# A decoder with two mixture layers on one core: indirect transfers broken up by sums, first fetches from another queue, the ready table built earlier

## The reference, cut to what matters

```python
# layer 0: 16 experts, 4 groups; a token takes 4 experts out of its 2 best groups
scores = softmax(xt @ Wg.T)
weights = take_along_axis(scores, topi)
h = silu(xt @ W1[e].T) * (xt @ W3[e].T)          # inner width 176
y = sum over the 4 chosen e of weights[e] * (h @ W2[e].T)
z = (silu(xt @ Ws1.T) * (xt @ Ws3.T)) @ Ws2.T    # two shared experts, width 352
x = layernorm(x + y + z)
# layer 1: 8 experts, a token takes 2
probs = softmax(gelu(x @ rw1) @ rw2)
Ye = gelu(x @ w1[e] + b1[e]) @ w2[e] + b2[e]     # inner width 1024
Ce = gelu(b1[e]) @ w2[e] + b2[e]                 # where a token has not chosen e
x = layernorm(x + sum over k, e of probs_k * (Ye or Ce))
```

## Time and profile before

| | us |
|---|---|
| median of three runs | 1445.8 |
| profiled execution | 1446.67 |
| its span in the profile | 1444.8 |
| TensorE matmuls busy | 1157.7 (80%) |
| TensorE weight loads busy | 924.1 (64%) |
| ScalarE busy | 521.8 (36%) |
| VectorE busy | 489.7 (34%) |
| GpSimd busy | 419.5 (29%) |

### The profile page before, as it was taken

One profiled execution on the slowest core, in us unless ns is written; L12 is line 12 of the kernel. 1 busy time (PEld: TensorE's weight loads), 2 busy tenths in 40 slices (PEclk: granted clock), 3 DMA queues, 4 the chain that ended last, 5 costly groups with the idle time before them and its releaser, 6 DMA issues. The chain is left out here.

```text
span 1444.8 us, 29452 instructions
## 1 busy us (share of the span) xinstructions
PE 1157.7 (80%) x10340; PEld 924.1 (64%) x10341; DVE 489.7 (34%) x1215; ACT 521.8 (36%) x1308; POOL 419.5 (29%) x521
## 2 busy tenths in 40 slices
PE   4988889868695069899947888888763599999998
PEld 2666767756353047676736667676542598989997
DVE  1255543555641012222233444554327300000223
ACT  2324433334131023333315555665430243333342
POOL 2022121121237731477441444121105300020143
PEclk9888988967698579999979999999755899999999
DMA  4011059900433323454440000000017564555573
GB/s 137 16 45 30 16 197 352 341 2 1 177 109 109 113 63 115 120 149 141 131 148 1 17 17 16 2 2 1 1 42 306 184 215 151 180 178 176 165 242 117
DMA packets 106677, 163.44 MB, mean 113 GB/s; under 512 B 16816, under 2 KB 86048, under 8 KB 104864
## 3 DMA queue, kind: packets, MB, share of 16 engines
q1 hardware_dynamic: 83344, 124.41, 26.4%
q0 software_dynamic: 9696, 26.75, 5.8%
q10 hardware_dynamic: 13536, 10.83, 2.3%
HBM read 100.87 MB, written 61.08 MB: 112 GB/s over the span
## 5 line engine op out<-in xcount | busy, mean ns | idle before, releaser
L2220 PE MATMUL bank<-m_XGT,m_w 128*128 128x128 f32 x1248 | 153.6, 283 | 4.4 <-issue 2.2
L2220 PEld LDWEIGHTS bank<-m_XGT,m_w 128*128 128x128 f32 x1248 | 149.2, 199 | 6.1 <-issue 4.5
L2234 PE MATMUL bank<-m_w,m_HT 128*128 x624 | 141.2, 379 | 0.0
L2071 ACT ACTIVATE m_HT<-bank,m_b 128x128 f32<-128x128 f32 x312 | 89.0, 369 | 108.3 <-PE bank L2220 73.2
L2234 PEld LDWEIGHTS bank<-m_w,m_HT 128*128 128x128 f32 x624 | 115.9, 191 | 14.2
L1311 PE MATMUL bank<-m_W,m_XGT 128*128 x316 | 110.8, 474 | 3.7 <-issue 2.8
L1015 POOL DMA_INDIRECT GA<-ys,r_pos x64 | 62.2, 972 | 101.6 <-DVE m_Y L1253 76.3
L2031 POOL DMA_INDIRECT m_GA<-ys,r_pos x32 | 31.6, 989 | 177.2 <-SPq L1989 168.5
L1184 ACT ACTIVATE m_XGT<-bank 128x256 f32<-128x256 f32 x79 | 30.3, 383 | 120.1 <-DVE m_Y L1253 88.4
L1311 PEld LDWEIGHTS bank<-m_W,m_XGT 128*128 128x128 f32 x316 | 55.4, 195 | 23.0 <-issue 6.3
L1133 POOL DMA_INDIRECT xs<-X,r_pos x64 | 62.4, 975 | 25.6 <-issue 15.2
(11 more groups left out here) (345 smaller groups left out, 2398.9 us busy)
## 6 DMA issues: line engine op xcount, KB each, us to landing
m_w<-in_m_w SPq DMA_DIRECT2D x47, 1024.0 KB, 5.4
m_XG<-xs SPq DMA_DIRECT2D x118, 128.0 KB
xs<-zeros SPq DMA_DIRECT2D x1, 10112.0 KB, 33.6
ys<-zeros SPq DMA_DIRECT2D x1, 10112.0 KB, 49.8
ys<-m_Y ACTq DMA_DIRECT2D x79, 128.0 KB
m_W<-in_w SPq DMA_DIRECT2D x2, 2816.0 KB, 14.5
xs<-zeros SPq DMA_DIRECT2D x1, 4992.0 KB, 47.9
ys<-zeros SPq DMA_DIRECT2D x1, 4992.0 KB, 34.2
```

Source lines behind the costliest of these rows:

```text
L2071: last = nc.scalar.activation(HT[:, b % 2, at, :], BU[i][:, c * P:(c + 1) * P], ACT.Gelu, bias=b1[:, b % WB, at:at + 1])
L2220: last = nc.tensor.matmul(BU[i][:, c * P:(c + 1) * P], w1[:, b, m, lo:lo + P], XGT[:, b % 2, m * P:(m + 1) * P], start=m == 0, stop=m == K ...
L2234: last = nc.tensor.matmul(BY[b % 2][:, 0:DIM], HT[:, b % 2, c, :], w2[:, bass.ds(e, 1), c, :], start=c == 0, stop=c == CH - 1)
```

## The change

In the first mixture layer:

- The scatter is issued two transfers at a time. Behind each pair GpSimd adds half a `Z` tile (128 of 256 columns) of the token tile before; behind the first pair of a tile it first waits until the token tile before has landed. The eight whole additions behind the scatter go.
- The gather of tile t+1 is issued one fetch at a time, each ahead of one of the four weightings of tile t.
- ScalarE issues the fetches of slot tiles 0 to 6 (0 to 3 ahead of its first copy, 4 to 6 between its next steps). SyncE starts with number 7, looks at `in_place` for one slot tile in four up to number 39, and for all after that waits once for the whole scatter.
- The steps of the ready table lie between the last up products of the shared experts.

In the second: `LAG` is 1; ScalarE issues the weights of slot tiles 0 to 3 and the rows of 0 to 3; SyncE starts with rows 4 and 5 and looks at `in_place` only in the first 12 steps of its loop; TensorE waits for the weights of the down products (`ld_w2`) ahead of its loop.

The diff without its context (the hunk of `layer1`, in which only an argument of `fetch_rows` goes, is left out):

```diff
@@ -956 +956 @@
-    def ready_on_dve(self, nc, dve, ident, req_bank, ready_bank, ahead):
+    def ready_on_dve(self, nc, dve, ident, req_bank, ready_bank, ahead, fill=None, fills=((), ())):
@@ -968 +968 @@
         self.req_step = do.k
+        for i in fills[0]:
+            fill(i)
         dve.wait_ge(self.counted, 4)
...
         self.ready_step = do.k
+        for i in fills[1]:
+            fill(i)
         dve.wait_ge(self.counted, 5)
...
-    def ready_on_pe(self, nc, pe, ones, ident, req_bank, ready_bank):
+    def ready_on_pe(self, nc, pe, ones, ident, req_bank, ready_bank, between=None):
         pe.wait_ge(self.steps.sem, self.req_step)
         nc.tensor.transpose(req_bank[0:TILES, 0:P], self.req[:], ident[:]).then_inc(self.counted, 1)
+        if between:
+            between()
         pe.wait_ge(self.steps.sem, self.ready_step)
@@ -987 +993 @@
-def tile_pipeline(engine, step, n, visits=()):
-    done = 0
+def tile_pipeline(engine, step, n, visits=(), done=0):
     for at, visit in (*visits, (n - PEEL, None)):
@@ -1009 +1014 @@
-def fetch_rows(nc, pool, fx, t, done):
+def fetch_row(pool, fx, t, k, done):
+    pool.indirect_dma_start(
+        out=fx.GA[:, t % 2, k, :], out_offset=None, in_=fx.ys,
+        in_offset=bass.IndirectOffsetOnAxis(ap=fx.pos0[:, t, k:k + 1], axis=0)).then_inc(done, 16)
+def fetch_rows(pool, fx, t, done):
     for k in range(TOP0):
-        pool.indirect_dma_start(
-            out=fx.GA[:, t % 2, k, :], out_offset=None, in_=fx.ys,
-            in_offset=bass.IndirectOffsetOnAxis(ap=fx.pos0[:, t, k:k + 1], axis=0)).then_inc(done, 16)
-def add_rows(nc, pool, fx, t, own):
+        fetch_row(pool, fx, t, k, done)
+def add_rows(nc, pool, fx, t, own, fetch=None):
...
     for k in range(TOP0):
+        if fetch:
+            fetch(k)
         last = nc.gpsimd.tensor_scalar(rows[:, k], rows[:, k], fx.wt0[:, t, k:k + 1], 1.0, ALU.mult, ALU.mult)
@@ -1037 +1048 @@
     POOL_GATES = 2 * SC + 1
+    FIRST, CHECKED = 7, 32
     with ExitStack() as mem:
@@ -1087 +1099 @@
-                def slot(j):
-                    return sp.value_load(r.tslot[0:1, bass.ds(j, 1)], min_val=0, max_val=NT - 1)
-                def load(j, b):
-                    need, s = sp.value_load(r.tneed[0:1, bass.ds(j, 1)], min_val=1, max_val=TILES), slot(j)
+                def load(j, b, checked=None):
+                    if checked is not None:
+                        need = sp.value_load(r.tneed[0:1, bass.ds(checked, 1)], min_val=1, max_val=TILES)
+                    s = sp.value_load(r.tslot[0:1, bass.ds(j, 1)], min_val=0, max_val=NT - 1)
                     sp.wait_ge(t_full, j + 1)
-                    sp.wait_ge(in_place, need)
+                    if checked is not None:
+                        sp.wait_ge(in_place, need)
                     sp.dma_start(XG[:, b, :].unsqueeze(1), slots[:, bass.ds(s, 1), :]).then_inc(ld_x[b], 16)
-                for j in range(7):
+                load(FIRST, FIRST % 4, FIRST)
+                with sp.Fori(0, CHECKED // 4) as i:
+                    for b in range(4):
+                        load(i * 4 + (FIRST + 1 + b), b, i * 4 + (FIRST + 4) if b == 0 else None)
+                sp.wait_ge(in_place, TILES)
+                with sp.Fori(0, (NT - FIRST - 1 - CHECKED) // 4) as i:
+                    for b in range(4):
+                        load(i * 4 + (FIRST + 1 + CHECKED + b), b)
+                for j in range(NT - (NT - FIRST - 1) % 4, NT):
                     load(j, j % 4)
-                def step(j, b, ahead):
-                    if follows(ahead, 7):
-                        load(j + 7, (b + 3) % 4)
-                tile_pipeline(sp, step, NT)
                 for b in range(2):
@@ -1128 +1142 @@
+                def add_shared(t, half):
+                    part = fx.X[:, t, half * P:(half + 1) * P]
+                    pool.wait_ge(z_used, t // 2 + 1)
+                    nc.gpsimd.tensor_tensor(part, part, Z[:, t, half * P:(half + 1) * P], ALU.add).then_inc(z_added, 1)
                 for t in range(TILES):
...
                             in_=fx.X[:, t, :], in_offset=None).then_inc(sent[t % 2], 16)
-                    if t:
-                        landed(t - 1)
+                        if t and k == 1:
+                            landed(t - 1)
+                        if t and k % 2:
+                            add_shared(t - 1, k // 2)
                 landed(TILES - 1)
-                pool.wait_ge(z_used, PAIRS)
-                for p in range(PAIRS):
-                    nc.gpsimd.tensor_tensor(fx.X[:, pair_tiles(p), :], fx.X[:, pair_tiles(p), :], Z[:, pair_tiles(p), :],
-                                            ALU.add).then_inc(z_added, 1)
-                pool.wait_ge(z_added, PAIRS)
+                for half in range(2):
+                    add_shared(TILES - 1, half)
+                pool.wait_ge(z_added, 2 * TILES)
                 own = fx.pool_steps
-                def gather(t):
+                def may_fetch(t):
                     pool.wait_ge(y_used, pool.value_load(r.ready[0:1, t:t + 1], min_val=3, max_val=NT + 2))
                     pool.sem_inc(due, 1)
-                    fetch_rows(nc, pool, fx, t, gathered[t % 2])
+                def fetch(t, k):
+                    fetch_row(pool, fx, t, k, gathered[t % 2])
                 pool.wait_ge(r.placed, 3)
-                gather(0)
+                may_fetch(0)
+                for k in range(TOP0):
+                    fetch(0, k)
                 for t in range(EARLY):
                     if t + 1 < EARLY:
-                        gather(t + 1)
+                        may_fetch(t + 1)
                     pool.wait_ge(gathered[t % 2], 16 * TOP0 * (t // 2 + 1))
-                    add_rows(nc, pool, fx, t, own)
+                    add_rows(nc, pool, fx, t, own, (lambda k: fetch(t + 1, k)) if t + 1 < EARLY else None)
@@ -1206 +1229 @@
+                def load(j, b):
+                    need = act.value_load(r.tneed[0:1, j:j + 1], min_val=1, max_val=TILES)
+                    s = act.value_load(r.tslot[0:1, j:j + 1], min_val=0, max_val=NT - 1)
+                    act.wait_ge(t_full, j + 1)
+                    act.wait_ge(in_place, need)
+                    act.dma_start(XG[:, b, :].unsqueeze(1), slots[:, bass.ds(s, 1), :]).then_inc(ld_x[b], 16)
+                act.wait_ge(r.placed, 2)
+                for j in range(4):
+                    load(j, j)
                 rows(0, 0)
+                load(4, 0)
                 rows(1, 1)
+                load(5, 1)
                 silu(0, 0)
                 rows(2, 2)
+                load(6, 2)
                 silu(1, 1)
@@ -1235 +1271 @@
                                ((POOL_GATES, POOL_GATES + 1), (POOL_GATES + 2,)))
-                for n in range(POOL_GATES + 3, SC * GROUPS):
-                    gated(n)
-                r.ready_on_dve(nc, dve, fx.ident[:], BU[0], BU[1], 2)
+                r.ready_on_dve(nc, dve, fx.ident[:], BU[0], BU[1], 2, gated,
+                               ((POOL_GATES + 3,), (POOL_GATES + 4,)))
@@ -1289 +1323 @@
                 r.order_on_pe(nc, pe, fx.ones, BU[0], BU[1], lambda: shared_up(3, (0,)))
-                shared_up(3, (1, 2))
+                shared_up(3, (1,))
+                r.ready_on_pe(nc, pe, fx.ones, fx.ident, BU[0], BU[1], lambda: shared_up(3, (2,)))
                 shared_down(2)
                 shared_down(3)
-                r.ready_on_pe(nc, pe, fx.ones, fx.ident, BU[0], BU[1])
@@ -1903 +1937 @@
     E2 = 2 * E1
-    HC, WB = CH // 2, 4
-    AHEAD, LAG, POOL_WRITES = 2, 4, PAIRS - 2
+    HC, WB, CHECKED = CH // 2, 4, 12
+    AHEAD, LAG, POOL_WRITES = 2, 1, PAIRS - 2
     with ExitStack() as mem:
@@ -1960 +1994 @@
-                def load(j, b):
-                    need, s = sp.value_load(r.tneed[0:1, bass.ds(j, 1)], min_val=1, max_val=TILES), slot(j)
+                def load(j, b, checked):
+                    if checked:
+                        need = sp.value_load(r.tneed[0:1, bass.ds(j, 1)], min_val=1, max_val=TILES)
+                    s = slot(j)
                     sp.wait_ge(t_full, j + 1)
-                    sp.wait_ge(in_place, need)
+                    if checked:
+                        sp.wait_ge(in_place, need)
                     sp.dma_start(XG[:, b, :].unsqueeze(1), slots[:, bass.ds(s, 1), :]).then_inc(ld_x[b], 16)
-                def load_w1(j, b, freed=None):
+                def load_w1(j, b, freed):
                     e = sp.value_load(r.texp[0:1, bass.ds(j, 1)], min_val=0, max_val=E1 - 1)
-                    if freed is not None:
-                        sp.wait_ge(h_gelu, freed)
+                    sp.wait_ge(h_gelu, freed)
                     sp.dma_start(w1[:, b].unsqueeze(2), io["m1_w1"][:, :, bass.ds(e, 1), :]).then_inc(ld_w1[b], 16)
...
                 sp.wait_ge(r.placed, 2)
-                for j in range(WB):
-                    load_w1(j, j)
-                    for i in ((0, 1), (2, 3), (), (4, 5))[j]:
```

(36 more changed lines are left out.)

## The result

The changed kernel took 1382.09 us (median of 4 runs, 1380.47 to 1389.18) against 1445.15 (4 runs, 1440.53 to 1446.75): a ratio of 0.9587, 95% interval 0.955 to 0.9624. The forecast was 1380, range 1362 to 1424. The total was met; two terms of its sum were not, with opposite signs.

A forecast was written before the change was run, and what follows sets the result against it. The prediction took GpSimd's long unbroken runs of indirect transfers, which freeze the other engines, to bound the two mixture-layer dips. 1446.7 - 56 (first layer) - 10 (second layer) = 1380.7, so 1380 us, range 1362 to 1424.

The forecast's parts named there:

- The freeze is what ends last, and breaks lift it: Both layers' dips: GpSimd's long unbroken run of indirect transfers holds the other engines; breaking it frees them.
- TensorE without a hole between 450 and 517: First layer, beside the scatter: sign that would show the forecast true, TensorE working on without a gap.
- First Y at 471.8: First layer: the first Y comes at 471.8 us, 56 us earlier than before.
- A pair takes 3.1 us: First scatter: two transfers and half a sum take 3.1 us, 6.2 a token tile; the scatter ends near 525.5.
- Broken pairs cost 0.1 us a transfer, 4 us in all (0 to 21): First layer's loop beside the scatter: about 42 transfers slow the other engines by 0.1 us each.
- Alternating gathers give back 4 us: First layer's loop: the run of eight gathers goes, as fetches alternate with sums, 4 us less.
- Net 0 for the loop: First layer, first to last Y: 4 us lost beside the scatter and 4 us regained from the gathers cancel.
- rival of a slow ScalarE queue: First layer: ScalarE's four fetches take 45 us instead of 6.7, gain about 25, time 1418; chance 0.14.
- GpSimd has 12 us to spare: First layer: the fetch of tile 11 can start at 645.5, let go at 657.4, so GpSimd stays hidden.
- Second layer 10 us: Second layer's start: third up product at 1135.8 against 1146.05, 10 us earlier, bounds 0 and 18.
- The gathers of the second layer keep their 7.82 us: Second layer: its run of eight gathers is untouched, so its 7.82 us on the chain of waits stay.
- rival of another cause: Both dips: something other than GpSimd's run holds the engines, time stays near 1446; chance 0.04.

The follow-up runs named there:

- a1_scatter_run: Changed kernel with the first layer's 64 scatter transfers unbroken again and all half sums of Z behind them: 1415.19 us.
- c4_break_alone: Kernel before the change, only its first scatter broken: behind every two transfers half a sum of Z and a second sum of that size: 1390.10 us, ratio 0.961.
- the fours: Changed kernel with four transfers of the first scatter, then one whole sum of Z, instead of two and half a sum: 1400.32 us.
- a2_gather_run: Changed kernel with the four gathers of the next token tile in the first layer issued in one run ahead of the sums: 1409.74 us.
- c3_long_sync: The kernel with the long breaks, its first seven row fetches of the first layer on SyncE's queue, none on ScalarE's: 1368.69 us against 1367.46.
- the long breaks: Changed kernel with a second sum of the same size, into a spare tile, behind every half sum of Z in the first scatter: 1367.46 us.

## Why the prediction was right, step by step

- *The freeze is what ends last, and breaks lift it.* Right: shown by `a1_scatter_run` one way, `c4_break_alone` the other. At the change's own spacing they lift it only in part: the sign "TensorE without a hole between 450 and 517" failed, with 32.11 us busy of the 51 from 466 to 517.
- *First Y at 471.8.* It came at 466.3. Z was done at 448.85 (forecast 452.5), the fetches began at 450.40 (453.1) and took 5.87 us for four (6.7), and the first Y followed 10.05 us behind them (12).
- *A pair takes 3.1 us.* 2.90: the first transfer took 0.98 behind 0.17, the half sum 0.46. The scatter ended at 516.3, not 525.5. It made the spacing closer than forecast, which is the wrong side.
- *Broken pairs cost 0.1 us a transfer, 4 us in all (0 to 21).* This term failed. The price was 28.9 us in one profile and 34.7 in the other (nine steps of 5.66, six of 8.23, against 2.45). I took the row of eight transfers in a row as the nearest and then 0.1 without a row. That row was read too low as well: 2.8 + 2 us over eight are 0.6 each and not at most 0.5, and VectorE's Y beside those eight came some 8 us late in all. (By the 3.1 us a pair 54 us also hold 35 transfers, not 42.) What counts is the spacing over a long stretch, and a pair at 1.452 us a transfer is near the fours' 1.426, where a slot tile took 11.3 us. At 1.63 us the 0.1 would have been enough: 25 steps of 2.55 us lose 2.4 us.
- *Alternating gathers give back 4 us.* It was 17. Before, the loop took 208.9 us for 78 steps, 17.7 more than 2.45 each; `a2_gather_run` and `c4_break_alone` with runs of gathers lose 16.4 and 16.9 behind the scatter, the kernels without them 0.2 to 4.6. I had counted only the run of eight, and too low, and left out the runs of four, beside most of which a step took 1.3 to 1.5 us longer before.
- *Net 0 for the loop.* +11.4; with the first Y 5.5 earlier than forecast, the first layer gave 50 instead of 56.
- *ScalarE's queue.* The rival of a slow ScalarE queue didn't come: four fetches took 5.87 us, not 45. (Its sum had a slip: a first Y near 510 gives 18 us, not 25.) But the queue brought nothing either, since SyncE does as well (`c3_long_sync`).
- *GpSimd has 12 us to spare.* Before the fetch of tile 11 it idled 7.58 us, not 12, and behind it there was next to nothing to spare. Its last sum ended at 679.96 and the copy of the last Y at 687.04, but in thirteen profiles SyncE's first transfer of the next block never came less than 2.2 us behind the last Y nor less than 9.3 behind the last sum; with the long breaks, where the last sum clearly bounds, it came 9.67 behind it. In the changed kernel it was 2.98 and 10.06: GpSimd stood at the edge of being the bound. What lies in the 9.3 us is not shown. The forecast asked only whether the last sum comes behind the last Y.
- *Second layer 10 us.* 12.3, and the two landings under load took 6.36 and 6.38 us (5 taken), the third 2.65 (2). The first up product was at 1070.95, 1120.5 in the old count (1120 forecast).
- *The gathers of the second layer keep their 7.82 us.* These were a piece of the chain and not TensorE's loss, as its timeline of the kernel before shows:

```profile
1283.21 0.61 PE L2220 MATMUL bank<-m_XGT,m_w 128*128 128x128 f32 x4
1291.74 3.79 PE L2234 MATMUL bank<-m_w,m_HT 128*128 x16
```

From these up products to the down products behind them it was 8.53 us, 5.0 more than for the slot tile before. In the changed kernel the same eight transfers (1212.80 to 1222.6) cost 2.6, which is 2.3 of the 4.3 us of the rest. The change didn't earn the 4.3: `c4_break_alone`, whose second layer is that of before, has 3.7 of them too. Why they vary is not shown.

So the total is right partly because errors cancel. Against the forecast's terms the first Y was 5.5 us better, the loop 11.4 worse (25 worse beside the scatter, 13 better behind it), the next block 0.4 worse, the second layer 6.6 better, of which most is seen without the change too (`c4_break_alone`). It is luck as well that the first profile had the cheapest of five stretches beside the scatter: in the second round the same kernel took 1400.36, 20 us above the forecast and still within its range.

The rival of another cause (time near 1446) is out by `a1_scatter_run` and `c4_break_alone`. The Trainium skill's rule (SBUF — State Buffer, "SBUF: two separate sides") that DMAs and engines don't slow each other speaks of the ports of SBUF. To take it for the whole time of the kernel, as the rival did, doesn't work here: with 64 transfers in a row ScalarE stood for 32.30 us (`a1_scatter_run`). Whether they meet at these ports or elsewhere, no run shows.

## What to carry to other kernels

When every engine idles with its data ready, look at what GpSimd issues: in this kernel a long stretch of indirect transfers 1.27 us apart stopped the others, and at 1.45, with a sum after every two, it still cost 29 to 38 us. Half a microsecond of a sum per pair was not enough. Space them (1.63 us each cost 2.4 us in all here), with useful sums where there are any and idle work where not, and then look whether GpSimd has become late. A total that comes out right doesn't vouch for its terms; only the rows of each do.

## What was not expected of the hardware

The price is steep in the spacing: 1.426, 1.452, 1.512 and 1.631 us a transfer gave 11.3, 5.7 to 8.8, 4.3 and 2.5 us a slot tile. With half the bytes a row the last copy of Z came as late (504.8 us against 510.7). Near the edge the same program ran at 1380 and at 1403 us, with TensorE's granted clock in the stalled stretch at 0.86 or 0.63.
